# Where ScalarE's diagonal copies and other passes stand around a unit's second decay

## The reference: what is computed

```
# block A: a 7x7 filter per image and channel, made from the image itself
key = softmax(x . K_w + K_b); filters = x . key
filters = relu(layernorm(conv0(filters)) * ln_w + ln_b); wgt = conv1(filters)
out = depthwise_conv7x7(x, wgt)
# block B: state-space scans at three resolutions, both directions
x, z = split(in_w . x); f1 = c1(x); f2 = conv2s2(f1); f3 = conv2s2(f2)
per level:  delta = softplus(dtw . dts + dtb); A = -exp(Al)
            h = h * exp(delta * A_n) + delta * B_n * x     (16 states n, along the positions)
            y = sum_n h_n * C_n + x * D;  y = layernorm(y)
out = out_w . ((y1 + up(y2 + up(y3))) * silu(z)) + out_b
```

## Time and profile before

| what | value |
|---|---|
| median of 3 runs | 4727.92 us (4725.44 to 4733.08) |
| the profiled execution | 4728.14 us, span 4726.3 us |
| busy, share of span | DVE 79%, POOL 71%, PE 66%, ACT 54% |
| one body of the loop, in the middle | 283.58 us |

### The profile page before, as it was taken

How to read it: one execution, slowest core, us unless ns; L and a number is a source line. 1 busy time by engine, 2 the same in 40 slices (tenths; PEclk the granted TensorE clock), 3 DMA queues, 4 the chain that set the end, 5 groups by cost and what they waited for, 6 DMA issues and landing times.

```text
span 4726.3 us, 51130 instructions
## 1 busy us (share of the span) xinstructions
PE 3118.1 (66%) x11852; PEld 1464.1 (31%) x11852; DVE 3732.3 (79%) x4199; ACT 2548.5 (54%) x6006; POOL 3341.5 (71%) x1908
## 2 busy tenths in 40 slices
PE   6876766667765767766667765777766667766411
PEld 4433333233332333333233332333333233332200
DVE  2188878788887888878788887888878788787787
ACT  3555556455555555556555555555556455554432
POOL 0088585786858778586786858678585786858787
PEclk8988878878887888778778887878878778888755
DMA  1045243443534445253443534445253443534544
GB/s 37 1 151 183 99 173 122 148 165 124 176 118 147 142 147 183 100 168 130 147 166 122 179 117 148 141 148 187 99 168 126 145 169 118 179 112 152 165 149 164
DMA packets 187259, 663.93 MB, mean 140 GB/s; under 512 B 22736, under 2 KB 24672, under 8 KB 186976
## 3 DMA queue, kind: packets, MB, share of 16 engines
q1 hardware_dynamic: 186976, 661.47, 41.1%
HBM read 639.76 MB, written 21.63 MB: 140 GB/s over the span
## 4 chain that ended last, share of the span: by engine, by line
issue 27%; DVE 25%; ACT 20%; POOL 13%; PE 12%; DVEq 1%; DMA 1%; POOLq 0%; SPq 0%; ACTq 0%
ACT diag L1087 10%; DVE h L581 6%; POOL bx L1334 6%; PE pconv L824 6%; DVE slot_c L572 5%; POOL y L1362 4%; ACT slot_b L1190 4%; DVE u L498 2%; POOL h L1357 2%; DVE o L637 2%; DVE rs L528 1%; DVE rs L520 1%; PE pm L772 1%; PE pm L764 1%; DVE xn L506 1%
## 5 line engine op out<-in xcount | busy, mean ns | idle before, releaser
L824 PE MATMUL pconv<-pad,diag 128*128 128x512 f16 x8064 | 2079.8, 416 | 300.6 <-DVE xn L506 175.1
L1362 POOL TENSOR_TENSOR y<-y,h 128x1024 f32<-128x1024 f32 (+2 forms) x672 | 1340.1, 1994 | 514.6 <-DVE h L581 491.0
L1190 ACT ACTIVATE slot_b<-delta,nega 128x512 f32<-128x512 f32 (+1 forms) x1280 | 801.1, 640 | 1155.4 <-DVE slot_c L572 1152.5
L824 PEld LDWEIGHTS pconv<-pad,diag 128*128 128x128 f16 x8064 | 835.1, 105 | 1526.1 <-issue 444.3
L1334 POOL TENSOR_TENSOR bx<-bb,u 128x1024 f32<-128x1024 f32 x512 | 1210.7, 2365 | 112.1 <-DVE slot_c L572 112.1
L572 DVE TENSOR_TENSOR_SCAN slot_c<-slot_b,slot_c,bx 128x512 f32<-128x512 f32 x512 | 663.7, 1296 | 507.5 <-ACT slot_b L1190 468.0
L572 DVE TENSOR_TENSOR_SCAN slot_c<-slot_b,bx 128x512 f32<-128x512 f32 (+1 forms) x1024 | 954.0, 956 | 128.7 <-ACT slot_b L1190 50.9
L581 DVE TENSOR_TENSOR h<-slot_c,cb 128x512 f32<-128x512 f32 x1280 | 860.8, 674 | 17.7 <-POOL y L1362 17.6
L1357 POOL TENSOR_TENSOR h<-h 128x512 f32<-128x512 f32 (+3 forms) x384 | 361.5, 941 | 98.3 <-DVE h L551 80.8
L1087 ACT ACTIVATE diag<-id,chi 128x128 f16<-128x128 f16 x1344 | 410.6, 387 | 2.9 <-PE pconv L824 2.9
L1087 ACT ACTIVATE diag<-id,clo 128x128 f16<-128x128 f16 x1344 | 410.6, 387 | 0.0
(11 more groups left out here) (166 smaller groups left out, 3784.1 us busy)
## 6 DMA issues: line engine op xcount, KB each, us to landing
bb<-bc_rows SPq DMA_DIRECT2D x592, 512.0 KB, 4.6
cb<-bc_rows SPq DMA_DIRECT2D x592, 512.0 KB, 4.1
xr<-in_x SPq DMA_DIRECT2D x16, 1024.0 KB, 5.0
out<-ob SPq DMA_DIRECT2D x16, 1024.0 KB
bc_rows<-rows SPq DMA_DIRECT2D x64, 64.0 KB, 1.6
w<-in_w SPq DMA_DIRECT2D x2, 256.0 KB
wc<-in_wc SPq DMA_DIRECT2D x2, 256.0 KB
bc_rows<-rows SPq DMA_DIRECT2D x16, 32.0 KB, 1.5
```

The source lines that it names most:

```text
L824: ins = nc.tensor.matmul(bank(pconv, k), w, pad[:, t, part, rows:rows + 16, dx:dx + W], start=first and m == 0, stop=last and m == 2)
L1190: ins = nc.scalar.activation(slot_b[:, o:o + w], delta[:, so + c:so + c + w], ACT.Exp, scale=nega[:, st, n0 + n:n0 + n + 1])
L1362: pool.tensor_tensor(yv, yv, src[:, 0] if len(src.shape) == 3 else src, ALU.add).then_inc(q_y.sem, 1)
```

## The change

On ACT, a row of 14 copies is cut in four parts over two units. Its 7 coarse copies are made in the unit where the row stood: 3 between the two decays and 4 behind the second. Its 7 fine copies are made in the unit after, again 3 and 4. Rows 0 to 3 begin in units 33, 34, 35 and 36; the fine copies of row 3 come in the bridge, ahead of row 4. `row_parts` walks over the rows of a unit. The second decay is moved ahead of all other passes of the unit but three: `gn_spread` and `b1` (units 34, 35), `chunk_log`, and `take_weights` in unit 33 stay ahead. The copies are the same in number and form. The wait of a row stands at its first part, its signal at its last.

```diff
-            def make_row(j, r):
+            def make_row(j, r, lo=0, hi=2 * KK):
+
                 t, dy = ROWS[r]
-                if r >= RING:
+                if lo == 0 and r >= RING:
                     act.wait_ge(row_done.sem, row_done.at(j, r - RING + 1))
-                elif not (isinstance(j, int) and j == 0):
+                elif lo == 0 and not (isinstance(j, int) and j == 0):
                     act.wait_ge(row_done.sem, row_done.at(j, 0))
...
+                for n in range(lo, hi):
+                    m, dx = divmod(n, KK)
+                    ins = nc.scalar.activation(diag[:, r % RING, m, dx, :], id16[:, :], ACT.Copy,
+                                               scale=(chi, clo)[m][:, t, dy * KK + dx:dy * KK + dx + 1])
+                if hi == 2 * KK:
+                    ins.then_inc(diag_made.sem, 1)
+
+            def row_parts(j, m, k, late):
+
+                for r in range(NR):
+                    for u in range(2):
+                        lo = 7 * u + 3 * late
+                        hi = lo + (4 if late else 3)
+                        if r < RING and m is not None and PREP + r + u == k:
+                            make_row(m, r, lo, hi)
+                        if r >= RING and j is not None and 0 < row_unit(r) == k - u:
+                            make_row(j, r, lo, hi)
@@ bridge
                 if m is not None:
+                    make_row(m, RING - 1, KK)
                     for r in range(RING, NR):
@@ unit
                     if 1 <= k < NU - 1:
                         decay(i, k + 1, 0)
+                if m is not None and k == PREP:
+                    take_weights(m)
+                    act.wait_ge(c_w.sem, c_w.at(m, 1))
+                row_parts(j, m, k, 0)
+                if i is not None:
+                    if 1 <= k < NU - 1:
+                        decay(i, k + 1, 1)
+                row_parts(j, m, k, 1)
+                if i is not None:
                     if k in CHUNK_PE:
                         chunk_exp(i, CHUNK_PE[k])
...
                     if k == PREP:
-                        take_weights(m)
                         prep(m)
-                if j is not None:
-                    for r in range(RING, NR):
-                        if row_unit(r) == k > 0:
-                            make_row(j, r)
-                if m is not None:
-                    if k == PREP:
-                        act.wait_ge(c_w.sem, c_w.at(m, 1))
-                    for r in FIRST_ROWS.get(k, ()):
-                        make_row(m, r)
-                if i is not None and 1 <= k < NU - 1:
-                    decay(i, k + 1, 1)
```

More of the change, by code:

```diff
@@ L1398 @@
 FIRST_TAPS = 2
-FIRST_ROWS = {PREP: (0,), PREP + 1: (1, 2), PREP + 2: (3,)}
 CHUNK_PE = {0: 2, 1: 3, 13: 4, 14: 5}
```

## The result

The changed kernel takes 4519.6 us in the median of its runs (4514.8 to 4529.0), 0.9561 times the kernel before (interval 0.9533 to 0.9588). The forecast was 4461 us, range 4400 to 4590: right in sign and inside the range, with 208 us gained of the 267 forecast. It lies at the very edge of the case that had been given 55% (4400 to 4520 us).

The account below looks back on a forecast made before the run. Waits set the time: no engine is busy over 79%, DVE's scans wait for ACT's decays. 11.8 + 0.7 + 1.2 + 4.4 = 18.1 us a body, times 14, plus ends: 267 us off 4728, 4461 us, range 4400 to 4590.

Parts of the forecast that it names:

- the case that had been given 55%: Whole kernel: the forecast gains come as summed, 4461 us, give or take, 4400 to 4520 us; chance 55%.
- Units 5 to 16: Front of a body: DVE's waits for second decays in units 9, 13 and 14 go, 11.8 us; bounds 7 and 16.
- Units 13 and 14: Second decays no longer stand behind the norm's root and row 8, or a softplus chunk: 4.7 and 2.6 us gained.
- the rule that the prediction weighed: Units 10 to 16: shared-port lock makes some three DVE passes wait for POOL's instruction, each losing up to 2.37 us.
- The gap of 1.3 us on ScalarE: Between a unit's two decays ACT has 1.3 us free: three copies (0.88 us) fit, fourteen don't.
- Unit 1, 0.7 us: Second decay no longer behind a chunk, so POOL's wait of 0.69 us for DVE goes: 0.7 us gained.
- Unit 27, 1.2 us: POOL's 1.22 us wait for image m's filters goes, as DVE delivers its part sooner: 1.2 us gained.
- Units 33 to 36: Tail: waits for decays shrink, so DVE reaches the bridge 8.2 us sooner; 1.9 us of unit 36's first wait stay.
- The bridge, 3.8 us given back: Behind unit 36: DVE waits 3.7 us for the norm's root, so 4.4 of 8.2 us gained are left.
- `copy_f` term: Tail: behind 22 copies, the projection's copy begins at 2205.1 against 2207.04, 1.9 us sooner.
- The slower case: Tail: image j's projection is late, TensorE's sums holding `b1`; costs 1.2 to 3.2 us a body, up to 4773 us; 6%.
- Half lost: Locked passes take 7.1 us a body, or the bridge keeps only 1.9 us: 4567 or 4496 us, both 4600; 30%.

Follow-up runs that it names:

- experiment 5: Norm's add and scale replaced by two scalar_tensor_tensor passes: in the changed kernel 4522.0 us; in the kernel with no diagonal copies in unit 36, 4448.0 us.
- experiment 2: Changed kernel with rows in parts but other passes ahead of the second decay: 4575.8 us; with passes moved but rows whole ahead of it: 4590.7 us.
- Experiment 6: Kernel before, with 9 spare copies on ScalarE ahead of `copy_f` in unit 36: 4729.7 us; with 18 spare copies: 4794.0 us.
- experiments 3 and 4: The former: see experiment 3. The latter: changed kernel with unit 36's copies moved to the bridge, 35 copies there, 4440.3 us; with 42 there, 4459.0 us.
- experiment 3: Changed kernel with two more taps of image m on TensorE in unit 36: 4460.7 us; instead with `copy_f` ahead of unit 36's diagonal copies: 4478.1 us.

## Why the prediction was right, and where it was off

- **Units 5 to 16, 11.8 us.** Measured 10.5. Up to the first sum of the convolution (unit 9's wait) 4.4 of 4.5 us came. Units 13 and 14 gave 6.1 of 7.3: the norm's passes meet GpSimd in another phase, L632 is 1.8 us longer and L630 0.6 us. This is the rule that the prediction weighed, with one pass hit hard instead of three; and it works both ways, L520's passes are 1.1 us shorter. Net it is some 1.2 us instead of 7.1. The Trainium skill (SBUF — State Buffer, "SBUF: two separate sides") has the shared port pair locked for the whole instruction; the trace agrees, 2.33 us of a pass that takes 0.41 while GpSimd stands idle, and both forms of experiment 5 pay.
- **The gap of 1.3 us on ScalarE.** Too strict (experiment 2): the second decay has 3.2 us, and 14 copies nearly fit. It did not enter the sum, as the parts fit by either count.
- **Unit 1, 0.7 us.** Not gained: the stretch from the first scan to the silu product is 0.5 us longer. GpSimd waits longer there for the transfer of `bb` (the rows of B). SyncE's and GpSimd's rows, before and after:

```profile
2232.89 0.40 SPq L414 DMA_DIRECT2D out<-ob  x1
2233.81 0.32 SPq L371 DMA_DIRECT2D bb<-bc_rows  x1
...
2239.43 2.35 POOL L1337 TENSOR_TENSOR bx<-bb,u 128x1024 f32<-128x1024 f32 x1 [2.46 <-DMA bb<-bc_rows]
```

```profile
2129.80 0.40 SPq L414 DMA_DIRECT2D out<-ob  x1
2130.69 0.33 SPq L371 DMA_DIRECT2D bb<-bc_rows  x1
...
2136.71 2.35 POOL L1348 TENSOR_TENSOR bx<-bb,u 128x1024 f32<-128x1024 f32 x1 [3.69 <-DMA bb<-bc_rows]
```

  SyncE issues this transfer behind the store of the output, which waits for VectorE's last passes on it, and not before GpSimd is done with `b`. Before, GpSimd was done at 2233.78, 0.9 us behind the store, and the transfer was issued 0.03 us later. In the changed kernel, where the root comes late for VectorE, the store is issued only at that moment (GpSimd is done at 2129.82), and the transfer is issued 0.9 us behind it and also takes 0.4 us longer. Experiment 6 bears it out body by body: 0.6 to 0.9 us behind in the bodies with the low clock, 0.02 to 0.03 in the five others. And with the tail undone, or with no copies in unit 36, the stretch is 0.2 us shorter than before. So some 0.7 of the 1.2 us missing here is the bridge's again, and 0.5 the term's own: it was sized too high.
- **Unit 27, 1.2 us.** Measured 1.9 up to the filters.
- **Units 33 to 36.** 8.2 forecast, 8.3 measured. The first scan of unit 36 waited 0.8 us, where 1.9 was foreseen.
- **The bridge, 3.8 us given back.** The failed step: "The chain from it to the root of the norm is one of TensorE and ACT by turns and moves as a whole". It moved and stretched, from 11.6 to 14.2 us in the mean, because the 22 copies ahead of `copy_f` let TensorE stand for 3.2 to 4.6 us (before, all 16 bodies together had 1.2 us) and its granted clock fell to 0.50. Measured, 5.4 us are given back. That the pause does it is shown by experiment 6, which puts it into the kernel before, and by 3 and 4, which take it out. The `copy_f` term itself held: 2.4 us sooner, counted from the filters, where 1.9 was forecast. There was luck in the size. The body that was read is one of the four whose chain took 12.8 us, with the root 2.6 us ahead of its use; by the mean of 11.6 the root was 3.7 us ahead of its use, and the same sum would have given back only 8.2 - 1.9 - 3.7 = 2.6 us, so the stretch cost more than the 1.6 us between 3.8 and 5.4 show. The 2.6 us by which the chain grew are 36 us in 14 bodies; the kernels of experiments 3 and 4 gained 59 and 79, with other things besides.
- **The other cases.** Waits of POOL for L581 fell by 183 us (200 forecast), those for the decays to 33 (under 150). The slower case, `b1` held by TensorE's sums, didn't come: `xg` began at once. The sign "DVE's passes beside POOL grow longer" did come, for L632. Half lost was the nearest of the rivals: 1.2 us went to locked passes and 1.6 in the bridge, where it had 7.1 and 2.5, but its reason for the bridge was the wait for `copy_f`, not a slower chain behind it.

## What to carry to other kernels

Look for what a producer's queue holds between two pieces that the slowest engine wants in turn; passes that nobody waits for go behind them, and a long run of small ones is best dealt out, but not ahead of the first piece of a chain that goes back and forth with TensorE. When a delay in such a chain is costed, look at how long TensorE will stand idle ahead of it: here the chain took 15.3 to 16.6 us at the lower clock in place of 11.1, more than the 3.2 us of delay. Moving the pause to another place in the same chain doesn't keep the clock up (experiment 3). And a cover in time has an edge: 35 copies in the bridge cost nothing, 42 cost 19 us.

## What the runs showed of the hardware

- TensorE's granted clock fell from 1.00 to 0.50 behind pauses of 3.2 to 4.6 us in 14 bodies of the changed kernel (L850 2.57 to 3.78 us), and of 3.0 and 3.7 to 3.8 us in eight of the 13 bodies of experiment 6. Directly behind pauses of up to 1.8 us it stayed at 1.00 (experiments 3 and 6), also behind 2.85 us once and 3.1 to 3.2 us five times. Yet it fell behind pauses of 2.4 us where `copy_f` stands first (0.51 in the window shown), and in four of 14 bodies of the kernel before it fell with no pause over 0.6 us in the chain ahead of it. The order of these pauses isn't that of the falls, so something beside the length of the last one counts; it stays open here. The Trainium skill (TensorE: Matmul & The Clock Gate, "Part 1: The HAM clock gate") has the clock set by how busy TensorE has just been, at one of two levels; the trace agrees, with 0.50 and 1.00 on either side of a pause.
- VectorE's pass L632 of 256 columns takes 0.41 us begun beside an idle GpSimd and 2.33 us begun beside its `bx`, inside its own time, so no view of waits shows it.
